# A fixed-point feed-forward layer: interleaving the steps of its rows and storing the output by batch

## The reference, cut to what matters

```python
def float2fix(x, mantissa_bits):              # round to multiples of 2^-8
    s = jnp.float32(2.0 ** mantissa_bits)
    return jnp.round(x * s) / s
def pwlin_gelu_basic(x, mantissa_bits_in, mantissa_bits_out):
    xq = float2fix(x, mantissa_bits_in)
    y = jnp.interp(xq, _PWL_X, _PWL_Y)        # 33 points of the exact GELU on [-4, 4]
    y = jnp.where(xq > 4.0, xq, jnp.where(xq < -4.0, 0.0, y))
    return float2fix(y, mantissa_bits_out)
h = float2fix(jnp.einsum('bsd,df->bsf', x, w1) + b1, 8)
h = float2fix(pwlin_gelu_basic(h, 8, 8), 8)
return float2fix(jnp.einsum('bsf,fd->bsd', h, w2) + b2, 8)   # x = x + this of layernorm(x)
```

## Time and profile before

| what | us |
| --- | --- |
| median of 3 runs | 2239.01 |
| lowest and highest of them | 2229.99 and 2239.91 |
| the profiled execution, its own time | 2236.96 |
| its span, first to last instruction | 2235.2 |

### The profile page before, as it was taken

How to read it: one execution, slowest core, us unless ns; L and a number is a source line. 1 busy time by engine, 2 the same in 40 slices (tenths; PEclk the granted TensorE clock), 3 DMA queues, 4 the chain that set the end, 5 groups by cost and what they waited for, 6 DMA issues and landing times. The chain is left out here.

```text
span 2235.2 us, 44143 instructions
## 1 busy us (share of the span) xinstructions
PE 1971.9 (88%) x17800; PEld 1086.3 (49%) x17800; DVE 1626.0 (73%) x2842; ACT 994.2 (44%) x1404; POOL 680.1 (30%) x704
## 2 busy tenths in 40 slices
PE   6799999999597366999999999999999999767896
PEld 3355555555344223455555555555555555434542
DVE  4689999999565773587777777777777776446676
ACT  2689899989310332233333333333333333202332
POOL 3344444444210450133333333233333332121010
PEclk9899999999698577999999999999999999888898
DMA  4332333232131301000000000000000000110400
GB/s 142 96 80 73 87 95 89 69 82 58 31 136 52 127 1 58 21 22 19 4 22 22 21 22 22 21 22 22 21 22 22 21 2 2 48 71 0 156 0 19
DMA packets 40090, 106.16 MB, mean 47 GB/s; under 512 B 19280, under 2 KB 21584, under 8 KB 33744
## 3 DMA queue, kind: packets, MB, share of 16 engines
q1 hardware_dynamic: 39888, 103.35, 15.1%
HBM read 75.42 MB, written 1.05 MB: 34 GB/s over the span
## 5 line engine op out<-in xcount | busy, mean ns | idle before, releaser
L1360 POOL TENSOR_SCALAR a1c_p_hi<-a1c_pf 128x512 f16<-128x512 f32 x272 | 202.5, 745 | 663.8 <-ACT a1c_pf L1416 620.2
L365 POOL TENSOR_SCALAR a0c_p_hi<-a0c_r 128x1024 f16<-128x1024 f32 x128 | 154.9, 1210 | 268.9 <-DVE a0c_r L465 266.0
L1385 ACT ACTIVATE a1c_k_hi<-PS 128x512 f16<-128x512 f32 x136 | 81.2, 597 | 326.8 <-PE PS L1222 326.8
L470 DVE TENSOR_TENSOR a0c_p_lo<-a0c_r,a0c_p_hi 128x1024 f16<-128x1024 f32 x128 | 201.5, 1574 | 0.9 <-POOL a0c_p_hi L365 0.9
L1565 DVE TENSOR_TENSOR a1c_p_lo<-a1c_pf,a1c_p_hi 128x512 f16<-128x512 f32 x272 | 197.9, 729 | 5.5 <-POOL a1c_p_hi L1360 5.5
L1392 ACT ACTIVATE a1c_v_hi<-PS 128x512 f16<-128x512 f32 x136 | 81.6, 600 | 258.8 <-PE PS L1232 206.0
L1416 ACT ACTIVATE a1c_pf<-PS,a_maskc 128x512 f32<-128x512 f32 x256 | 175.1, 685 | 47.7 <-PE PS L1727 40.1
L1508 DVE CUSTOM_DVE_ANT_0 a1c_junk<-PS,a1c_maskr 128x512 bf16<-128x512 f32 x256 | 175.7, 686 | 18.4
L465 DVE TENSOR_TENSOR a0c_r<-PS,a0c_r 128x1024 f32<-128x1024 f32 x128 | 155.3, 1213 | 34.1 <-ACT a0c_r L411 34.0
L1483 DVE SCALAR_TENSOR_TENSOR a1c_k_lo<-PS,a1c_k_hi 128x512 f16<-128x512 f32 x136 | 93.8, 689 | 106.6 <-ACT a1c_k_hi L1385 106.6
L1490 DVE SCALAR_TENSOR_TENSOR a1c_v_lo<-PS,a1c_v_hi 128x512 f16<-128x512 f32 x136 | 93.9, 691 | 86.6 <-ACT a1c_v_hi L1392 85.1
(11 more groups left out here) (358 smaller groups left out, 4784.7 us busy)
## 6 DMA issues: line engine op xcount, KB each, us to landing
a_cf<-in_ctxT SPq DMA_DIRECT2D x16, 1024.0 KB, 5.1
a0c_ks<-a0c_k_hi SPq DMA_DIRECT2D x128, 128.0 KB, 2.3
a1c_cf<-in_ctx SPq DMA_DIRECT2D x16, 1024.0 KB, 4.8
a0c_ks<-a0c_k_lo SPq DMA_DIRECT2D x64, 128.0 KB, 2.4
f_w<-in_w SPq DMA_DIRECT2D x4, 1024.0 KB, 8.7
f_w<-in_w SPq DMA_DIRECT2D x1, 4096.0 KB, 19.6
s1q_w<-in_L1a_wT SPq DMA_DIRECT2D x3, 1024.0 KB, 7.7
w_gate_raw<-in_w_gate SPq DMA_DIRECT2D x1, 2816.0 KB, 10.4
```

Source lines behind the costliest of these rows:

```text
L365: nc.gpsimd.tensor_scalar(p_hi[:, u % 4, :], r[:, u % 4, :], 1.0, 0.0, ALU.mult, ALU.add)\
L470: nc.vector.tensor_tensor(p_lo[:, u % 4, :], r[:, u % 4, :], p_hi[:, u % 4, :], ALU.subtract)\
L1360: nc.gpsimd.tensor_scalar(p_hi[:, v % 4, :], pf[:, v % 2, :], 1.0, 0.0, ALU.mult, ALU.add)\
```

## The change

Nothing outside `fixed_point_ffn_1` and the final store is touched.

- **PE.** `output` lags `hidden` by 4 rows and not 3 (LAG). The semaphore `outputs` goes up once for each batch of the last row and not once after the fourth.
- **The work of a row.** Values of `u`, `c` and `k` are now in units of 64/256, the width of a segment. POOL's step goes: `k` is one DVE instruction (add, add). max(u, 1024) goes from DVE to ACT as a Relu, with a bias from a [128,1] tile. DVE has 8 instructions for each row and not 9, ACT 5 and not 4, POOL none and not one.
- **The order.** DVE does, in step n, `whole(n - 2)`, `segment(n)`, `between(n - 1)`. ACT does `grid(n + 1)`, `ends(n)`, `nearest(n - 1)`. `u` has 4 buffers, the others 3.
- **The waits at the start.** ACT's first instruction waits for the scaled `b1` alone.
- **The end.** DVE waits for each batch of its own. SP stores each batch, 256 KB, when it is done, from within the block; the semaphores are cleared after the last store has landed.

```diff
+    GRID = 64.0
+    GROUND = ROUND / GRID
     ONE = 256.0
+    LAG = 4
...
-        R = 2
-        u, c, k, g0, g1 = (m.sb(n, [P, R, D]) for n in ("u", "c", "k", "g0", "g1"))
+        u = m.sb("u", [P, 4, D])
+        c, k, g0, g1 = (m.sb(n, [P, 3, D]) for n in ("c", "k", "g0", "g1"))
...
         with nc.Block() as block:
+            @block.sync
+            def _(sp):
+                for b in range(B):
+                    sp.wait_ge(x_done, b + 1)
+                    sp.dma_start(out[b], g.x[:, b, :]).then_inc(stored, 16)
+                sp.wait_ge(stored, 16 * B)
...
-                    if f == FT1 - 1:
-                        mm.then_inc(outputs, 1)
-                for f in range(FT1 + 3):
+                        if f == FT1 - 1:
+                            mm.then_inc(outputs, 1)
+                for f in range(FT1 + LAG):
                     if f < FT1:
                         hidden(f)
-                    if f >= 3:
-                        output(f - 3)
+                    if f >= LAG:
+                        output(f - LAG)
...
+                act.wait_ge(biased, 1)
+                def grid(f):
+                    act.wait_ge(product, f + 1)
+                    if f >= 4:
+                        act.wait_ge(y_done, f - 3)
+                    nc.scalar.activation(u[:, f % 4, :], g.PS[:, f % 4, :], ACT.Identity, bias=b1s[:, f:f + 1],
+                                         scale=ONE / GRID).then_inc(u_done, 1)
...
+                def ends(f):
+                    i = f % 3
+                    act.wait_ge(k_done, f + 1)
+                    if f >= 3:
+                        act.wait_ge(y_done, f - 2)
+                    nc.scalar.activation(g0[:, i, :], k[:, i, :], ACT.Gelu, scale=0.25, bias=low[:, 0:1])\
+                        .then_inc(g0_done, 1)
+                    nc.scalar.activation(g1[:, i, :], k[:, i, :], ACT.Gelu, scale=0.25, bias=high[:, 0:1])\
+                        .then_inc(g1_done, 1)
+                    nc.scalar.activation(u[:, f % 4, :], u[:, f % 4, :], ACT.Relu, scale=GRID, bias=knee[:, 0:1])\
+                        .then_inc(hm_done, 1)
...
+                def nearest(f):
+                    act.wait_ge(y4_done, f + 1)
+                    nc.scalar.activation(g0[:, f % 3, :], g0[:, f % 3, :], ACT.Copy, scale=ONE, bias=ROUND)\
+                        .then_inc(yr_done, 1)
+                grid(0)
                 act.wait_ge(based, 3)
...
-                for f in range(FT1):
-                    first(f)
-                    ends(f)
-                    last(f)
+                for n in range(FT1 + 1):
+                    if n + 1 < FT1:
+                        grid(n + 1)
+                    if n < FT1:
+                        ends(n)
+                    if n >= 1:
+                        nearest(n - 1)
...
-                nc.gpsimd.memset(quarter[:], 0.25).then_inc(based, 1)
-                for f in range(FT1):
-                    i = f % R
-                    pool.wait_ge(c_done, f + 1)
-                    nc.gpsimd.tensor_scalar(k[:, i, :], c[:, i, :], 1.0 / 64, -31.5 / 64, ALU.mult, ALU.add)\
-                        .then_inc(ka_done, 1)
+                nc.gpsimd.memset(low[:], -ROUND / 4).then_inc(based, 1)
+                nc.gpsimd.memset(high[:], 0.25 - ROUND / 4).then_inc(based, 1)
+                nc.gpsimd.memset(knee[:], -1024.0).then_inc(based, 1)
...
+                nc.vector.tensor_scalar(b1s[:], b1[:], ONE / GRID, None, ALU.mult).then_inc(biased, 1)
+                nc.vector.tensor_scalar(b2s[:], b2[:], ONE, None, ALU.mult).then_inc(biased, 1)
...
+                def segment(f):
+                    U, C, K = u[:, f % 4, :], c[:, f % 3, :], k[:, f % 3, :]
                     dve.wait_ge(u_done, f + 1)
-                    nc.vector.tensor_scalar(U, U, ROUND, ROUND, ALU.add, ALU.subtract).then_inc(h_done, 1)
+                    nc.vector.tensor_scalar(U, U, GROUND, GROUND, ALU.add, ALU.subtract).then_inc(h_done, 1)
...
+                    if f >= 3:
+                        dve.wait_ge(td_done, f - 2)
+                    nc.vector.tensor_scalar(C, U, 1024.0 / GRID, -1024.0 / GRID, ALU.min, ALU.max)\
+                        .then_inc(c_done, 1)
                     dve.wait_ge(c_done, f + 1)
-                    nc.vector.tensor_scalar(U, U, 1024.0, None, ALU.max).then_inc(hm_done, 1)
-
-                    dve.wait_ge(ka_done, f + 1)
-                    nc.vector.tensor_scalar(K, K, ROUND, ROUND, ALU.add, ALU.subtract).then_inc(k_done, 1)
+                    if f >= 3:
+                        dve.wait_ge(g1_done, f - 2)
+                    nc.vector.tensor_scalar(K, C, -31.5 / GRID, ROUND, ALU.add, ALU.add).then_inc(k_done, 1)
...
+                    nc.vector.scalar_tensor_tensor(out=C, in0=K, scalar=ROUND, in1=C, op0=ALU.subtract,
+                                                   op1=ALU.subtract).then_inc(t_done, 1)
...
+                def between(f):
+                    C, G0, G1 = c[:, f % 3, :], g0[:, f % 3, :], g1[:, f % 3, :]
                     dve.wait_ge(g1_done, f + 1)
                     nc.vector.tensor_tensor(G1, G1, G0, ALU.subtract).then_inc(rise_done, 1)
...
                     nc.vector.tensor_tensor(G1, G1, C, ALU.mult).then_inc(td_done, 1)
...
+                    nc.vector.tensor_tensor(G0, G0, G1, ALU.subtract).then_inc(y4_done, 1)
...
+                def whole(f):
                     dve.wait_ge(yr_done, f + 1)
                     dve.wait_ge(hm_done, f + 1)
...
+                    nc.vector.scalar_tensor_tensor(out=y[:, f, :], in0=g0[:, f % 3, :], scalar=ROUND,
+                                                   in1=u[:, f % 4, :], op0=ALU.subtract, op1=ALU.add)\
+                        .then_inc(y_done, 1)
+                for n in range(FT1 + 2):
+                    if n >= 2:
+                        whole(n - 2)
+                    if n < FT1:
+                        segment(n)
+                    if 1 <= n <= FT1:
+                        between(n - 1)
+                dve.wait_ge(biased, 2)
                 for b in range(B):
+                    dve.wait_ge(outputs, b + 1)
                     nc.vector.tensor_tensor(o[:, b, :], g.PS[:, 4 + b, :], b2s[:], ALU.add).then_inc(o_done, 1)
...
-        for layer in (self_attention_1, fixed_point_ffn_1):
-            layer(nc, g, d)
-            clear_semaphores(nc)
-        stored = m.sem("stored")
-        with nc.Block() as block:
-            @block.sync
-            def _(sp):
-                sp.dma_start(out.rearrange("b p n -> p b n"), g.x[:]).then_inc(stored, 16)
-                sp.wait_ge(stored, 16)
+        self_attention_1(nc, g, d)
+        clear_semaphores(nc)
+        fixed_point_ffn_1(nc, g, d, out)
+        clear_semaphores(nc)
```

More of the change, by code:

```diff
@@ L2051, in fixed_point_ffn_1 @@
         w1, w2 = m.sb("w1", [P, KT, F1]), m.sb("w2", [P, FT1, D])
[L2052 removed]
+        b1, b1s, b2, b2s = m.sb("b1", [P, FT1]), m.sb("b1s", [P, FT1]), m.sb("b2", [P, D]), m.sb("b2s", [P, D])
+        low, high, knee = m.sb("low", [P, 1]), m.sb("high", [P, 1]), m.sb("knee", [P, 1])
         w2_in, b_in = m.sem("w2_in"), m.sem("b_in")
@@ L2061, in fixed_point_ffn_1 @@
         y = m.sb("y", [P, FT1, D])
-        R = 2
-        u, c, k, g0, g1 = (m.sb(n, [P, R, D]) for n in ("u", "c", "k", "g0", "g1"))
+        u = m.sb("u", [P, 4, D])
+        c, k, g0, g1 = (m.sb(n, [P, 3, D]) for n in ("c", "k", "g0", "g1"))
         o = m.sb("o", [P, B, D])
-        based, product, u_done, h_done, c_done, ka_done, k_done, t_done = (m.sem(n) for n in (
-            "based", "product", "u_done", "h_done", "c_done", "ka_done", "k_done", "t_done"))
+        based, biased, product, u_done, h_done, c_done, k_done, t_done = (m.sem(n) for n in (
+            "based", "biased", "product", "u_done", "h_done", "c_done", "k_done", "t_done"))
         g0_done, g1_done, rise_done, td_done, y4_done, yr_done, hm_done, y_done = (m.sem(n) for n in (
             "g0_done", "g1_done", "rise_done", "td_done", "y4_done", "yr_done", "hm_done", "y_done"))
-        outputs, o_done, or_done, x_done = m.sem("outputs"), m.sem("o_done"), m.sem("or_done"), m.sem("x_done")
+        outputs, o_done, or_done, x_done, stored = (m.sem(n) for n in ("outputs", "o_done", "or_done", "x_done", "stored"))
         with nc.Block() as block:
+            @block.sync
[4 more added lines that the diff above has]
+                sp.wait_ge(stored, 16 * B)
             @block.tensor
@@ L2098, in _ @@
             @block.scalar
             def _(act):
-                act.wait_ge(based, 3)
[L2101 to L2122, removed]
-                for f in range(FT1):
-                    first(f)
-                    ends(f)
-                    last(f)
+                act.wait_ge(biased, 1)
[5 more added lines that the diff above has]
+                                         scale=ONE / GRID).then_inc(u_done, 1)
@@ L2139, in _ @@
                 dve.wait_ge(b_in, 32)
```

(8 more changed lines are left out.)

12 lines of the change are left out of this document (1 added, 11 removed).

## The result

| kernel | median of the runs, us | lowest to highest | profiled execution | its span |
| --- | --- | --- | --- | --- |
| before | 2237.11 (5 runs) | 2229.99 to 2239.91 | 2236.96 | 2235.2 |
| changed | 2217.01 (5 runs) | 2211.44 to 2219.14 | 2217.67 | 2215.9 |

The ratio is 0.9909, with a 95% interval of 0.9887 to 0.9932. The forecast was 2217.0, in a range of 2207 to 2224.

What follows compares the result with a forecast made beforehand. PE was taken to set the pace at 6.87 us a row. Gains of 16.9 us on PE, 2.6 from the first batch's early start and 1.6 from the store sum to 21.05 us; forecast 2217, range 2207 to 2224.

Steps and rivals of the forecast that it cites:

- The bound: Middle of the last stage: PE sets the pace, 6.87 us a row; closing its gaps gives at most 16.9 us.
- The ring: DVE and ACT steps of one row, with a bare wait for `nearest`: 5.44 us, under PE's 6.87.
- Check one: First output: `w2` 0.9 us and `y(0)` 2 us to spare; the 2.3 us gap and 1.7 of slow clock go.
- Check two: Middle rows: PE wants `y(n)` over 20 us after `hidden(n)`, against about 7 of steps; each wait is met.
- Check three: Last rows: `y(15)` ready at 2198.0, wanted at 2202.0, 4 us to spare; the last three gaps and slow clock go.
- Check four: Tail: DVE starts at 2202.9 when batch 0 is done and ends 7.24 us later at 2210.15, 19.45 us gained so far.
- the store: End: the last 256 KB store lands in 2.6 us, between bounds of 2.3 and 4.3; 1.6 us gained.
- A: Start: `w2` lands 1 to 2 us later and PE idles, about 2220; chance 0.14 together with two other rivals.
- B: ACT: the Relu brings two more table loads a row, 2219; chance 0.14 together with two other rivals.
- C: End: the store gains nothing, 1.7 us lost, 2219; chance 0.14 together with two other rivals.
- D: Rows: PE at half clock behind waits of 2.3 us or more; eight rows at half speed give 2272; chance 0.03.
- E: Change not on the path: only start or end heals, gain 8 to 17 us, 2222 to 2229; chance 0.08.

Runs made afterwards that it cites:

- steps_not_interleaved: Changed kernel, but ACT and DVE do all steps of one row before any of the next; 2216.56 us, ratio 0.9913 to before.
- old_steps_interleaved: Changed kernel with the old steps back: shift of `k` on GpSimd, its rounding and the maximum on DVE; 2215.50 us, ratio 0.9902 to before.
- max_on_dve: Changed kernel with the maximum back on DVE in place of the Relu on ACT; 2218.44 us, ratio 0.9921 to before.
- tail_only: Kernel before with only the changed tail: outputs signalled and stored batch by batch, semaphores cleared after the store; 2230.52 us, ratio 0.9973.
- order_only: Changed kernel with the old tail: outputs signalled once after the fourth batch, one store in its own block; 2221.00 us, ratio 0.9931 to before.
- grid_last: Changed kernel with ACT doing `grid(n + 1)` after `ends(n)` and `nearest(n - 1)`, not first; 2216.99 us, ratio 0.9914 to before.
- by_batch_warm: grid_last plus outputs of the last two rows batch by batch and 30 unread transposes on PE before the layer norm's; 2212.47 us, ratio 0.9889 to before.
- lag4_only: Kernel before with the lag of `output` behind `hidden` at 4 rows in place of 3, nothing else; 2235.77 us, ratio 1.0004.

## Why the prediction was right

**The bound.** PE at 6.87 us a row was read rightly as what limits the stage once its gaps are closed. steps_not_interleaved, old_steps_interleaved and max_on_dve put the ring at 6.19, 6.24 and 5.77 us, and none moves the time by more than its interval or the stage by more than 0.2 us. In the kernel before it was not yet the bound: its ring took 7.11 us a row, and PE ran at 6.87 only while its lead of three rows lasted. In tail_only that lead is used up early, and the output groups are 7.1 us apart from 2153.11 us on.

**The ring.** Forecast 5.44, measured 5.42. The bare wait for `nearest` is there at 0.69. The guess of 6.2 for the steps in series was right as well (6.19).

**Check one.** `w2` and `y(0)` made PE wait no more. `y(0)` came at 2112.75, 2.3 us later than I had it. Of this, 0.9 is the later `b1` (scaled at 2102.87 and not 2101.97). The rest is the half clock: I let `grid(1)` start behind `grid(0)`, and at half clock its product was done only for a start at 2105.15. PE was late by nearly as much and wanted `y(0)` at 2115.19, so 2.4 us were spare (forecast 2). order_only, at full clock, is the case that was worked out: `y(0)` is there 14.8 us after the first hidden record (forecast 2110.4 - 2095.35 = 15.05), with 2.4 us to spare.

**Check two.** Right for PE, wrong for ACT and DVE. I had DVE waiting for `grid` with everything behind it in flow, and 0.69 us of wait in `whole` in every row. In fact ACT stands at `grid(n + 1)` with `nearest(n - 1)` behind it. `y(13)` is there 4.0 us after the last hidden group has given way to the outputs; in grid_last it is there 0.4 us before (2186.18 against 2186.61).

**Check three.** This is the step that was mis-sized: 4 us to spare for `y(15)`, and 0.9 measured (2203.55 against 2190.72 + 32 * 0.4292 = 2204.45). The forecast held because 0.9 is still more than nothing, and not because this step was right. grid_last, which takes that wait away, has the 10 us after `hidden(15)` that the prediction had worked out.

**Check four and the store.** DVE works 7.25 us from 2205.58 to 2212.83 (forecast 7.24). The store lands in 2.0 us, less than both bounds I gave (2.3 and 4.3): 128 KB between two tiles was no lower bound for 256 KB to memory. The estimate by the Trainium skill, DMA: Bandwidth & Descriptors, on the cost components of one transfer, of 2.6 us was too high by as much as mine; the measurement decides. The four stores were issued 1.79 us apart and did not pile up: between 2212.80 and 2213.20 us, just before the last one moved its data, the DMA engines moved nothing.

**The sum.** The span ends at 2215.9 and not 2214.15. PE started 0.7 us later, which is noise of the layers ahead, and lost 1.9 us at half clock at the start (19.32 us and not 17.4 for 40 records). This loss is a term that the prediction had put at nothing: it took the 13.97 us of the first 32 records from the one profile of before, and nine of the twelve profiles have about 15.9 there. The store gave 0.6 back, and what comes behind it took 0.3 less than put down. 0.7 + 1.9 - 0.6 - 0.3 = 1.7. That the median hit the forecast to the decimal is luck: the profiled execution was forecast at 2215.9 and took 2217.67, 1.8 more, and the 1.1 us added for the gap between the profiled run and the median, which in the end was the other way (the median is 0.7 under the profiled run), covered most of it. The median of before has also moved, from 2239.01 to 2237.11 with two more runs, so the gain was forecast at 22.0 us and is 20.1.

**The rivals.** A: the loads were in time here, and no wait is put down to `w2` in order_only and by_batch_warm either, where PE was at full clock. B: after `std` the stage has one table load (L2127, at 2105.86), as before, with 16 Relus between the Gelus; the Trainium skill, ScalarE: Activation LUTs, in its section on table sets, has Relu in every set, and the trace agrees. C: the store gained more than forecast. D: PE was slow for the first 4 us only, at the start of the stage, and not after a wait in the rows. Its premise, that a wait of 2.3 us or more is followed by a half-speed stretch, is not sure: in lag4_only the groups behind waits of 2.45, 3.41 and 3.41 us took 3.70 us each. E: lag4_only heals the gap at the start alone. The prediction had put a gain of 8 to 17 us on one healed end; this one gives nothing, because the gap at the start was not on the path of the kernel before, and PE only waited longer at the end.

## What to carry to other kernels

Find the engine that is the bound of the stage when all waits are met, and work out the ring of the others against it. The ring must be shorter than that, and the last tile's result must still be there in time; what it is shortened beyond this bought nothing here. A lag in front of a ring that is too long only moves the gap to the end. On an engine that works in order, an early step that waits for the bounding engine delays every later step queued behind it: put it last in the steady rows, and look at the first tile apart, where the same order makes the first result late. A stage's own length, from its first instruction to the end of the span, tells differences of 2 us that the total time of this kernel hides, but only if the clock at its start is compared too. And when an engine is kept busy so that its clock stays up, count from what its real work waits for: the extra instructions can hold that work back by as much as the clock gives.

## What the runs showed of the hardware

The same gap of PE does not always cost the same. Gaps of 3.4 us before an 8-record output group stand in three profiles: in before the groups behind them took 5.40 and 5.40 us, in lag4_only 3.70, 3.70 and 5.40, in tail_only 6.47 and 3.70. At full clock such a group takes 3.60. So the clock fell behind four of seven gaps of one length. In lag4_only the last two of them have the same ahead of them, a gap of 3.41 us and a group of 3.70, and only the second was followed by the slow clock. The shorter gaps are no different: behind 2.31 us in before the group took 5.30, behind 2.45 in lag4_only 3.70. The 5.4 us that the prediction put on slow clock behind gaps is therefore the loss of one execution and not a constant. The start of the stage is of the same kind: nine of twelve profiles began it at half clock and lost 1.9 to 2.1 us; before and order_only began it at full clock although PE had done the same ahead of it, and so did by_batch_warm, where the extra transposes kept PE busy ahead of it.
